# Four stage boundaries of an attention kernel rewritten: three queues for the projection's stores, an early bias table, first maxima on the scores' banks, and heads joined in a pipeline

## The reference

```python
qkv = q @ in_proj_weight.T + in_proj_bias              # projection
bias_r = einsum('bhid,rd->bhir', qh, rel_pe)           # 129 relative positions, clipped at 64
bias = take_along_axis(bias_r, rel, axis=-1)
attn = softmax(qh @ kh.T + bias)
out = (attn @ vh) @ out_w.T + out_b                    # join of the heads
x = layernorm(x + out)                                 # first norm, kept for the end
for l in range(2):
    x = layer(x, wqkv[l], ...)                         # window attention and feed-forward
x = layernorm(first_norm + x)
```

## Time and profile before

| | |
|---|---|
| median of 3 runs | 5409.09 us (5408.53 to 5411.06) |
| profiled execution | 5405.9 us |
| its span | 5404.2 us |
| PE busy | 5081.9 us (94% of the span) |
| DVE busy | 4165.8 us (77%) |
| ACT busy | 3071.8 us (57%) |
| POOL busy | 997.2 us (18%) |
| DMA | 248.33 MB, mean 46 GB/s |

### The profile page before, as it was taken

The page is one execution under the profiler, slowest core; times in us unless marked ns, Lnnn a source line. Parts: engine busy times, 40 slices in busy tenths (PEclk is TensorE's granted clock), DMA queues, the critical chain, the costliest instruction groups (busy, mean ns, idle before and its releaser), DMA issues. The chain is left out here.

```text
span 5404.2 us, 114950 instructions
## 1 busy us (share of the span) xinstructions
PE 5081.9 (94%) x33760; PEld 2659.9 (49%) x33760; DVE 4165.8 (77%) x8817; ACT 3071.8 (57%) x4539; POOL 997.2 (18%) x791
## 2 busy tenths in 40 slices
PE   8499999999999999999999999986799989899989
PEld 4233333333333333333333333333688867788866
DVE  6388888888888888888888888942677744677755
ACT  4166666666666666666666666640456522556521
POOL 0212111111111121121111111101233210333210
PEclk9599999999999999999999999985899999899999
DMA  6312212212122122122122111110200000000010
GB/s 206 80 52 57 57 52 57 57 49 57 51 57 58 51 57 55 50 56 58 52 57 57 49 50 51 56 53 31 67 0 0 12 5 0 18 0 0 1 40 24
DMA packets 199610, 248.33 MB, mean 46 GB/s; under 512 B 60574, under 2 KB 128484, under 8 KB 197732
## 3 DMA queue, kind: packets, MB, share of 16 engines
q1 hardware_dynamic: 194388, 226.76, 14.3%
q0 software_dynamic: 5136, 20.45, 2.1%
HBM read 210.72 MB, written 36.18 MB: 46 GB/s over the span
## 5 line engine op out<-in xcount | busy, mean ns | idle before, releaser
L770 DVE TENSOR_REDUCE group_max<-shared_ps 128x1 f32<-128x512 f32 x4096 | 2700.5, 686 | 417.9 <-PE shared_ps L498 316.3
L651 ACT ACTIVATE probs<-scores 128x1024 f32<-128x1024 f32 x2048 | 1986.8, 1022 | 985.4 <-DVE scores L746 706.7
L498 PE MATMUL shared_ps<-keys,max_queries 96*128 96x512 bf16 x4096 | 1431.4, 384 | 5.3 <-DVE group_max L770 3.5
L525 PE MATMUL scores<-queries,keys 98*128 98x512 bf16 (+3 forms) x4096 | 1224.6, 370 | 4.6 <-ACT probs L651 2.6
L540 PE MATMUL out_ps<-probs,values 128*17 128x512 f32 x8192 | 1079.1, 599 | 5.2 <-ACT probs L651 0.6
L498 PEld LDWEIGHTS shared_ps<-keys,max_queries 96*128 96x128 bf16 x4096 | 393.4, 96 | 1116.2 <-DVE group_max L770 619.4
L231 POOL TENSOR_TENSOR near_window<-near_bias,one_f 128x1536 bf16<-128x1536 f32 x128 | 351.5, 2746 | 2755.7 <-DVE max_parts L764 2148.8
L525 PEld LDWEIGHTS scores<-queries,keys 98*128 98x128 bf16 x4096 | 366.1, 98 | 304.9 <-ACT probs L651 60.6
L551 PE MATMUL shared_ps<-block_q,block_table 96*128 96x32 bf16 x4096 | 271.9, 233 | 79.6 <-POOL block_q L435 79.6
L551 PEld LDWEIGHTS shared_ps<-block_q,block_table 96*128 96x128 bf16 x4096 | 233.2, 114 | 176.9 <-issue 137.7
L1207 POOL TENSOR_TENSOR norm<-norm,layer_expo 128x16 f32<-128x16 f32 x64 | 186.3, 2910 | 707.5 <-DVE norm L1593 707.5
(11 more groups left out here) (195 smaller groups left out, 5743.9 us busy)
## 6 DMA issues: line engine op xcount, KB each, us to landing
keys<-k_parts SPq DMA_DIRECT2D x384, 96.0 KB, 2.1
values<-v_wide SPq DMA_DIRECT2D x128, 272.0 KB, 2.6
keys<-k_parts SPq DMA_DIRECT2D x384, 64.0 KB, 2.0
keys<-k_parts SPq DMA_DIRECT2D x128, 132.0 KB, 2.4
k_parts<-part SPq DMA_DIRECT2D x96, 128.0 KB
queries<-q_parts SPq DMA_DIRECT2D x768, 16.0 KB, 1.6
max_queries<-q_parts SPq DMA_DIRECT2D x768, 16.0 KB, 1.6
keys<-k_parts SPq DMA_DIRECT2D x384, 32.0 KB, 1.8
```

The costliest lines, as they stand in the source:

```text
L498: mm = pe.matmul(bank, max_queries[par][:, t * P:(t + 1) * P], keys[par][0:ROWS, (t + TPC * g) * P:(t + TPC * (g + 1)) * P], start=True, s ...
L525: mm = pe.matmul(out[:, 0:cut], keys[par][:, tile * P:(tile + 1) * P], queries[par][:, 0:cut], start=True, stop=True)
L651: act.activation(probs[s % 4][:], scores[s % 2][:], ACT.Exp).then_inc(exp_done, 1)
L770: dve.tensor_reduce(group_max[par][:, k:k + 1], bank, AX.X, ALU.max).then_inc(max_read, 1)
```

## The change

Nothing is changed in the loop over the 128 steps of the attention or in the windows and batches of the layers. At the four boundaries:

- *Projection.* SP stores the near variants (12 parts a chunk), POOL the two far ones of k (6 parts a chunk) in between its loads of x, and ScalarE the last span of values. The value bias and its row of ones go. `v_stage` is no longer filled as a whole by DVE; POOL sets its column of ones and the two key buffers' extra rows. TensorE waits for the weights alone. DVE cuts the table ahead of its first split and places it after chunk 1; SP writes its rows after chunk 0's stores.
- *Set-up.* POOL loads `head_q` of head 0 first. SP loads keys ahead of queries, ScalarE loads the first `max_queries`. The first 36 score groups, those that need no window of biases, go to the four halves of the `scores` banks, in turns with the biases; then eight near ones there, the last bias block, and four on shared banks.
- *Join.* Weights, bias and identity are loaded during the attention. Tiles are transposed straight from `tokens`, two tiles ahead, with four buffers on each side. The output bias plus `v_bias @ out_w.T` is made once and added to x by POOL, in eight pieces, as x arrives in eight loads. Statistics are worked out in five groups, and ScalarE normalises between its copies. The layers' first weights are loaded, rounded and split here. `first_norm` is stored in five pieces.
- *Layers.* What was loaded in the join is not loaded again. POOL picks the first tile before its fills, and TensorE turns it before it waits for `set_up` and weights. DVE waits for the five stores ahead of its first residual add.

The core of the diff:

```diff
@@ projection
+        FAR = (3, 5)
+        def store_parts(eng, n, v, signal):
+            unit = VARIANTS[v][0]
+            eng.wait_ge(low_done, n * 6 + v + 1)
+            heads = slice(GROUP * (unit % 2), GROUP * (unit % 2 + 1))
+            side = n * CH + N if v in FAR else n * CH
+            parts = q_parts if unit < 2 else k_parts
+            for which in range(3):
+                eng.dma_start(parts[heads, which * D:(which + 1) * D, side:side + CH],
+                              part[:, n % 2, which, v, :]).then_inc(signal, 16)
...
+            load_x(0)
+            load_x(1)
+            pool.memset(v_stage[:, :, :, D:VW], 1.0).then_inc(ones_set, 1)
...
+            for n in range(CHUNKS):
+                store_parts(pool, n, FAR[0], far_stored[n % 2])
+                if n + 2 < CHUNKS:
+                    load_x(n + 2)
+                store_parts(pool, n, FAR[1], far_stored[n % 2])
...
-            pe.wait_ge(consts_in, 64)
-            pe.wait_ge(ones_set, 2)
+            pe.wait_ge(weights_in, 16)
...
-                        pe.matmul(out, x_in[:, par, k, t * P:(t + 1) * P],
-                                  weights[:, k, 2 * E:3 * E], start=k == 0, stop=False)
-                    mm = pe.matmul(out, ones_row[:], v_bias[:], start=False, stop=True)
+                        mm = pe.matmul(out, x_in[:, par, k, t * P:(t + 1) * P],
+                                       weights[:, k, 2 * E:3 * E], start=k == 0, stop=k == KE - 1)
...
+                    act.wait_ge(near_stored[n % 2], NEAR_STORES * (n // 2))
+                    act.wait_ge(far_stored[n % 2], FAR_STORES * (n // 2))
...
+            store_v(act, CHUNKS - 1, last_v_stored)
+            act.wait_ge(last_v_stored, 32)
@@ set-up, POOL and TensorE
+            load_head_q(0, 0)
...
             for b in range(CHUNKS):
                 copy_block(0, b, 0)
+                if b == 3:
+                    load_head_q(1, 1)
...
+            for j in range(FIRST):
+                first_max(j)
+            for e in range(CHUNKS):
                 for half in range(2):
-                    if e:
-                        pe.wait_ge(bias_read, e * 2 + half - 1)
-                    make_bias(e, e % 2, half)
+                    first_bias(e, half)
+                    for j in range(2):
+                        first_max(FIRST + 4 * e + 2 * half + j)
@@ join
+            def turn(t):
+                if t >= 4:
+                    pe.wait_ge(tile_kept, t - 3)
+                for k in range(KE):
+                    mm = pe.transpose(turned[t % 4][:, k * P:(k + 1) * P], tokens[:, t, k * P:(k + 1) * P], ident_f[:])
+                mm.then_inc(tile_turned, 1)
...
+            for t in range(TILES):
+                if t + AHEAD < TILES:
+                    turn(t + AHEAD)
+                join(t)
...
+            for t in range(TILES):
+                keep(t)
+                for past in NORM_AFTER.get(t, ()):
+                    normalise(past)
+            act.wait_ge(early.staged_in, 16)
+            act.activation(early.wqkv_hi[:].rearrange("p k n -> p (k n)"), early.w_stage[:], ACT.Copy
+                           ).then_inc(early.w_rounded, 1)
+            for t in range(1 + max(max(past) for past in NORM_AFTER.values()), TILES):
+                normalise(t)
```

578 lines of the change are left out of this document (327 added, 251 removed).

## The result

The changed kernel takes 5237.34 us (median of 4 runs, 5232.81 to 5242.16) beside 5410.08 for the kernel before on the same chip: a ratio of 0.9678, interval 0.9662 to 0.9695. The profiled execution took 5233.09 us, 172.8 less than that of before, where 217.5 were forecast. It is faster, but above the range given: 5192 was forecast and 5232 was its end.

A forecast was written before the change was run, and what follows sets the result against it. TensorE bounds the main loop (3349.3 of 5404.2 us), left alone; gains lie in four boundaries of 451.7 us. Savings 37.4 + 41.6 + 115.7 + 22.8 = 217.5 take 5405.9 to 5188.4, forecast 5192 us, range 5178 to 5207.

The forecast's parts named there:

- part 1: Projection: earlier TensorE start, no one-row bias products, stores on three queues; 159.9 to about 122.5 us, minus 37.4.
- The term of 0.35 us: Projection: DMA time of each of a chunk's 18 part stores, taken as 0.54 of the 0.656 us issue time.
- The three queues do nothing: Rival, projection: issue time is not what counts, the stage stays 159.9 us, total 5229 us; chance 0.04.
- 140 as the upper end: Projection's upper bound in us: chunk 4's parts queue behind V on SP, ScalarE and TensorE wait, the clock falls.
- Part 2: Set-up of the attention: `head_q` first, early table, maxima in turns with biases; 89.6 to about 48 us, minus 41.6.
- Part 3: Join: no gaps for TensorE, full clock, 1.3 us a tile; 173.7 to about 58 us, minus 115.7.
- 7 + 39: Join: 7 us at half clock, then 30 tiles of 1.3 us at full clock, 39; summed there to 46.5 us.
- The stall on ScalarE's first normalisation: Join: ScalarE waits for POOL's bias add to x, stalling TensorE about 3 us, perhaps 3 more in clock.
- beside that tail: Join's end: ScalarE rounds the layers' weights (2.76 us) and DVE splits them alongside the tail, where POOL's power takes 1.0 us.
- The rival of a low clock: Rival, join: clock stays low, 93 us in place of 58, total 5227 us; chance 0.19.
- Part 4: Start of the layers: weights prepared in the join; 28.5 to about 5.7 us, minus 22.8, bounds 4 and 9.
- starved: Rival, projection: DVE's work holds off POOL's stores; stage 145 us, total 5215, chance 0.03; kernel slower than before, 0.01.

The follow-up runs named there:

- p_probe: Changed kernel with the projection's stores made again behind it in six phases, on one, two or three queues, with nothing else running; 5434.41 us.
- p_rows128: Changed kernel with the scratch laid out part by part, each part store's destination 128 rows, and keys read 16 rows at a time; 5194.58 us.
- p_all_sp: Changed kernel with the far stores back on SP's queue, POOL keeping only loads of x and ScalarE the last values; 5231.27 us.
- p_one_queue: Changed kernel with every store of the projection on SP's queue, the last values too; 5233.98 us.
- best3: Changed kernel with three parts merged per store (128 rows outermost), keys read 16 rows at a time, join's weight cut behind the last tiles; 5191.42 us.
- p_v_end: Changed kernel with the first two value spans stored by SP after the last chunk's parts, not after chunks 3 and 5; 5224.89 us.
- j_ahead0: Changed kernel with no tile of the join turned ahead, so TensorE waits for the copy in each tile; 5246.44 us.
- p_probe2: Changed kernel with extra phases on SP alone behind the projection: 36 parts, all values in 2, 4, 8 and 64 DMAs, then x; 5409.22 us.

## Why the prediction missed, step by step

**The step that failed is part 1, "Issue no longer binds; the DMA engines do. Their work is 0.64 of 159.9 us, 102 us", with its "stores of 0.35 us (0.54 of 0.656)".** It read a share of 0.54 in the earlier trace rows as engines that were idle 46% of the time, and took it that more queues would fill them to 1.04. The probe shows that they would not: parts alone hold the share at 0.50 to 0.59 on one, two or three queues. The 0.656 us of the earlier trace rows it read rightly as SP's price of issuing (0.64 on idle engines in the probe), but not as the bound: a second limit, the engines' 0.68 to 0.76 us a part store, lay at the same place or above, so that lifting the first gained nothing. The term of 0.35 us is the price of a store spread over all engines: at p_rows128's 342 GB/s, 128 KB are 0.38 us, and there the stage ended at 123.7, near the forecast 122.5. In the changed kernel a store took nearly twice that, and the estimate above, 155 to 167 us, holds the measured 164.9. Without POOL's stores the stage ended at 159.6 and 160.4 (p_all_sp, p_one_queue), 2 to 5 us earlier than in the runs with the changed kernel's projection; why, is open. That best3 took 5191.42 us, next to the forecast of 5192, is luck: it has other stores and another join.

Why 0.50: eight heads outermost. p_rows128 takes that away, and the half share goes with it. The views used here carry no engine number, so eight engines of sixteen were not counted one by one; the share, the cure at equal size, and the keys' slow reads with 3 or 2 outermost agree on it. The Trainium skill has the rule, in DMA: Bandwidth & Descriptors, sections Why a DMA increments its semaphore by 16 and not by 1 and Rules for kernel authors: the number of engines is the largest up to 16 that divides the slowest dimension of both sides. By that rule heads give 8, three parts 3, and 128 rows 16; the runs agree (share 0.50, and 1.06). The prediction cited another section of the same page, that queues of several engines save only issue time, and argued that this trace was the exception. It was not: the rival "The three queues do nothing" (5229 us, chance 0.04) is what happened, with a stage of 164.9 us for its 159.9.

**The bounds of part 1.** 140 as the upper end rested on the same 0.35 us and so could not hold 164.9. The stall that it priced at 17.5 us, chunk 4's parts behind the values, did occur: 19.02 us of ScalarE's and 11.78 of TensorE's waiting. Removing most of it (p_v_end) gave 11 us, to 154.0, since the engines bound the stage besides.

**Part 2, set-up: right mechanism, a term mis-sized.** The first bias came 13.9 us in, not 9.9: `head_q` landed 12 us after its issue began where 8.3 were counted (the issue and a landing as before); the keys' loads now run beside it, which probably is why, though no run takes them apart. From there sixteen biases and two maxima took 1.75 us a turn at half clock, 28 in all, near the upper estimate of 28.6 rather than the 26 taken. 4.0 + 2.0 of the 6.6 us.

**Part 3, join: right to 0.2 us, partly by luck.** Tile pitch 1.085 us, better than 1.3; the clock was still full from the attention when the join began (the four matmuls of the value bias took 1.03 us here and 2.08 in j_ahead0), and 0.88 on average. The sum itself is off by a little: 7 + 39 is 46, not 46.5. The stall on ScalarE's first normalisation was 6.54 us, not 3, since `join_shift` came late. POOL's eight pieces took 18.49 us, less than the 20 counted, but they began 5.7 us into the join, behind the load of x that the prediction had "always ahead of POOL", and TensorE with its short tiles was there sooner:

```profile
3570.07 1.03 PE L1057 MATMUL join_joined<-out_weights,join_v_bias 128*128 128x256 f32 x4
```

```profile
3574.52 18.49 POOL L1017 TENSOR_TENSOR x_rows<-x_rows,out_bias 128x1024 f32<-128x1024 f32 x8 [4.83 <-DMA x_rows<-in_x]
```

```profile
3594.08 2.05 PE L1049 MATMUL join_joined<-out_weights,join_tile_T 128*128 128x256 f32 x4 [6.54 <-DVE tokens L1095]
```

The tail's power took 4.12 us, not 1.0, beside the subtraction that the prediction let run "beside that tail" at no price. The gains and misses cancel. The rival of a low clock did not come; in j_ahead0 it did not come with gaps either, nor with a low clock at the start. Why the kernel before stayed at 0.51 with gaps of 0.55 us a tile is open: its one-row bias product, absent in all these runs, was not tried by itself.

**Part 4 and the rest.** 4.5 us for 5.7, inside the bounds. The main loop is unchanged to 0.1 us. POOL's stores were not starved: 0.59 us each.

## What to carry to other kernels

A DMA share that sat at a half while a queue was full of work was not spare capacity here: look at the outermost dimension of the stores, then at what issues them. An issuing engine that is busy without a gap may be one of two limits at the same height; ask what the next limit allows before lifting the first. Change the scratch layout for the writer only after looking at each reader's walk; here the writer's cure cost the main loop 75 us until the reads were cut along the same rule. And test "more queues" first by its opposite: one queue did as well as three, which one run could have told.

## What the runs showed of the hardware

- 128 KB stores with eight heads outermost: 0.775 us each at a share of 0.50; with 128 rows outermost, beside values and x, the engines reached 342 GB/s at 1.06 (p_rows128).
- SP's issue of a 128 KB store took 0.64 us with eight heads outermost, on idle engines (p_probe), and 0.50 with 128 rows outermost (p_rows128).
- 8.9 MB of values took 23.8 us in 2 DMAs with pieces of 2176 bytes, 26.8 in 4 with 1088, 32.8 in 8 with 544 (p_probe2); pieces and number change together here. In 64 DMAs with pieces of 1088, SP's issue, 0.49 us each, set the time, 33.1 us.
- Loads of x in pairs, 4.2 MB, took 20.8 us at a share of 0.60, where each pair waited for the landing of the one before (p_probe2).
- The clock stayed up through gaps of 0.47 us in each tile of 1.8 us, and rose from half in spite of them (j_ahead0).
- A POOL operation of 1.01 us took 4.12 beside a two-input VectorE operation of 3.35.
